# Pacing the gathers of the third and fourth batch on GpSimd by steps of the turn

## The reference

```python
x = x + tanh(g_xattn[0]) * L0_xattn(ctx, layernorm(x), ...)
x = x + tanh(g_ffn[0]) * L0_ffn(layernorm(x), ...)        # 64 experts, 8 per token
x = x + tanh(g_xattn[1]) * L1_xattn(layernorm(x), ctx, ...)  # 16 heads, causal
x = x + tanh(g_ffn[1]) * L1_ffn(layernorm(x), ...)        # 8 experts, 2 per token, and a shared one
```

```python
out = sum_j w8[token, j] * expert_out[row_of(token, j)]
```

## The kernel before

| step | engine, line | reports |
|---|---|---|
| normed input flipped, copied to XB | PE L707, ACT L947 | e_xt |
| queries, high part copied | PE L714, ACT L952 | e_hi_q |
| queries spread over the rows, copied to QS | PE L626, ACT L957 (two), DVE L1411 (two) | e_qs, 4 a turn |
| maxima of the scores, 8 units | PE L729 to L732, DVE L1417 | e_max |
| 16 heads: scores | PE L757 to L759 | e_s2 |
| 16 heads: exponentials | ACT L970 | e_exp, 16 a turn |
| average of 4 heads, four times | PE L747 | e_av |
| sums copied to OS | ACT L972 | e_os |
| flipped, divided | PE L768, DVE L1434, L1437 | e_ot, e_ont |
| flipped, copied to ON | PE L776, ACT L977 | e_on |
| output projection, added | PE L781, DVE L1446 | e_y, e_x3 |
| normed output flipped, copied to XB3 | PE L796, ACT L984 | e_xt3 |

## Time and profile before

### The profile page before, as it was taken

One profiled execution on the slowest core, in us unless ns is written; L12 is line 12 of the kernel. 1 busy time (PEld: TensorE's weight loads), 2 busy tenths in 40 slices (PEclk: granted clock), 3 DMA queues, 4 the chain that ended last, 5 costly groups with the idle time before them and its releaser, 6 DMA issues.

```text
span 597.7 us, 9231 instructions
## 1 busy us (share of the span) xinstructions
PE 424.5 (71%) x2738; PEld 356.9 (60%) x2738; DVE 345.3 (58%) x1053; ACT 185.0 (31%) x377; POOL 147.2 (25%) x156
## 2 busy tenths in 40 slices
PE   5353643303999999997137727899588988898796
PEld 3232532203998889985125514797368966886686
DVE  4897865395344444442357812488546976492664
ACT  4112210101233333433611412525235172526431
POOL 4117676572000000002776370000720000000000
PEclk9998565555999999998557775799878998899999
DMA  7997222175799999994332130000310000000000
GB/s 249 425 410 323 90 97 80 70 278 171 214 305 321 321 312 326 378 399 145 105 89 72 35 100 9 1 2 5 96 45 18 1 2 0 18 1 3 2 18 19
DMA packets 36789, 82.96 MB, mean 139 GB/s; under 512 B 6032, under 2 KB 16144, under 8 KB 34960
## 3 DMA queue, kind: packets, MB, share of 16 engines
q1 hardware_dynamic: 22896, 55.83, 26.8%
q0 software_dynamic: 6144, 16.79, 8.7%
q10 hardware_dynamic: 7712, 9.90, 4.6%
HBM read 50.44 MB, written 31.92 MB: 138 GB/s over the span
## 4 chain that ended last, share of the span: by engine, by line
PE 54%; issue 13%; DVE 12%; POOL 7%; ACT 6%; another core or an unknown queue 4%; DMA 3%; SPq 1%; DVEq 0%; POOLq 0%; ACTq 0%
PE PS L563 11%; PE PS L573 7%; POOL slots_in L439 6%; PE PS L652 5%; PE PS L626 3%; PE PS L550 3%; PE PS L729 2%; PE PS L665 2%; PE PS L666 2%; PE PS L667 2%; PE PS L781 2%; DVE WORK L1069 2%; DVE TOP L1065 2%; PE PS L714 2%
## 5 line engine op out<-in xcount | busy, mean ns | idle before, releaser
L449 POOL DMA_INDIRECT GB<-slots_out,IDXG x64 | 68.8, 1074 | 213.1 <-SPq L367 139.8
L563 PE MATMUL PS<-XTE,WR 128*128 128x128 f32 (+2 forms) x512 | 80.4, 301 | 0.0
L439 POOL DMA_INDIRECT slots_in<-XNA,IDX x64 | 64.9, 1014 | 39.0 <-issue 31.3
L563 PEld LDWEIGHTS PS<-XTE,WR 128*128 128x128 f32 x512 | 71.3, 195 | 0.3 <-ACT XTE L875 0.2
L1257 DVE TENSOR_TENSOR HE<-SGE,PS 128x128 f32<-128x128 f32 (+2 forms) x64 | 19.9, 311 | 68.1 <-ACT SGE L884 64.9
L573 PE MATMUL PS<-WR,HE 128*80 128x256 f32 (+2 forms) x198 | 53.3, 380 | 0.3 <-DVE HE L1257 0.3
L665 PE MATMUL PS<-XH,WGH 128*128 128x256 f32 x160 | 51.3, 320 | 0.0
L875 ACT COPY XTE<-PS 128x256 f32<-128x256 f32 (+2 forms) x64 | 26.3, 410 | 73.4 <-PE PS L550 73.4
L652 PE MATMUL PS<-WD,XW 128*128 128x256 f32 x160 | 43.5, 396 | 5.8 <-DVE TH L1335 5.8
L550 PE MATMUL PS<-CF,XE 80*128 80x80 f32 (+2 forms) x198 | 28.5, 257 | 26.2 <-DMA XE<-slots_in 26.2
L666 PE MATMUL PS<-XL,WGH 128*128 128x256 f32 x160 | 45.9, 287 | 0.0
(11 more groups left out here) (226 smaller groups left out, 825.0 us busy)
## 6 DMA issues: line engine op xcount, KB each, us to landing
WR<-in_wexp SPq DMA_DIRECT2D x64, 384.0 KB
slots_in<-GB SPq DMA_DIRECT2D x12, 1024.0 KB, 18.1
XE<-slots_in SPq DMA_DIRECT2D x24, 160.0 KB, 4.4
slots_out<-OE ACTq DMA_DIRECT2D x24, 160.0 KB, 4.3
XE<-slots_in SPq DMA_DIRECT2D x29, 128.0 KB, 4.6
slots_out<-OE ACTq DMA_DIRECT2D x29, 128.0 KB, 4.9
WGU<-in_wgu SPq DMA_DIRECT2D x1, 2560.0 KB
XE<-slots_in SPq DMA_DIRECT2D x11, 192.0 KB, 3.6
```

The lines of the kernel that those rows point to most:

```text
L439: pool.indirect_dma_start(out=xs, out_offset=bass.IndirectOffsetOnAxis(ap=IDX[:, t, j:j + 1], axis=0), in_=XNA[:, t, :], in_offset=None, b ...
L449: pool.indirect_dma_start(out=GB[:, t % BT, j, :], out_offset=None, in_=ys, in_offset=bass.IndirectOffsetOnAxis(ap=IDXG[:, t, j:j + 1], ax ...
L563: last = mm(psGE[place % 2][:, a, 0:cap(place)], W13[:, k, a, :], XTE[:, place % 2, k, 0:cap(place)], start=(k == 0), stop=(k == KC - 1))
```

## The change

The change gives `gather` an optional function that is called before every second of its 8 DMAs. For batches 2 and 3 it makes GpSimd wait for a step of the turn. Batches 0 and 1 are issued as before.

| pair of DMAs | first tile of batch b waits for | second tile waits for |
|---|---|---|
| 0 | (as before: gb_used) | XB3 copied, turn b-2 (and gb_used) |
| 1 | 8 exponentials of turn b-2 | XB copied, turn b-1 |
| 2 | OS copied, turn b-2 | high part of the queries copied, turn b-1 |
| 3 | ON copied, turn b-2 | QS complete, turn b-1 |

```diff
-            def gather(t):
+            def gather(t, pace=None):
                 for j in range(TOP0):
+                    if pace and j % 2 == 0:
+                        pace(t, j // 2)
                     pool.indirect_dma_start(out=GB[:, t % BT, j, :], out_offset=None, in_=ys,
...
+            def pace(t, pair):
+
+                at = t // BT - 2
+                if t % BT == 0:
+                    if pair == 1:
+                        pool.wait_ge(S["e_exp"], at * NH + NH // 2)
+                    elif pair == 2:
+                        pool.wait_ge(S["e_os"], at + 1)
+                    elif pair == 3:
+                        pool.wait_ge(S["e_on"], at + 1)
+                elif pair == 0:
+                    pool.wait_ge(S["e_xt3"], at + 1)
+                elif pair == 1:
+                    pool.wait_ge(S["e_xt"], at + 2)
+                elif pair == 2:
+                    pool.wait_ge(S["e_hi_q"], at + 2)
+                else:
+                    pool.wait_ge(S["e_qs"], (at + 1) * 4 + 4)
...
-                    gather(b * BT + i)
+                    gather(b * BT + i, pace if b >= 2 else None)
```

## The result

| | time, us (lowest to highest, runs) | ratio to before, 95% |
|---|---|---|
| before | 600.24 (598.06 to 602.74, 4) | |
| changed | 570.74 (565.74 to 577.02, 4) | 0.950 [0.945, 0.956] |

The later runs put a condition on this result: the kernel before takes 591 to 600 us in three sittings (a sitting is one round of runs on one chip) and 566 to 567 us in four others, and in one of those four the changed kernel was timed too, with no gain.

The account below looks back on a forecast made before the run. TensorE reports late beside unbroken gathers were taken to bound turns 0 and 1. Savings 14.6 + 8.2 less 8.3 that stays gave 14.5 us, so 599.5 became 585.0, forecast 586 at the median; range 577 to 597 us.

Parts of the forecast that it names:

- the place and the mechanism: Turns 0 and 1: TensorE's work is reported 2 to 8 us late while gathers stream; ceiling 22.8 us.
- signs asked for: Changed profile: paired gathers, turn 0 remote waits about 3 us, turn 1 near 31 us, no combine waiting for a DMA.
- Term 4: Seven pairs per batch moved later: cost 0, with about 11 us of slack before combine needs them.
- term 3: Lateness that stays: 2.5 us in turn 0, 2 in turn 1, 3.8 for 12 lone pairs; 8.3 us.
- Rival A: Relief nearly complete: pairs cause no lateness, only turn 1's four in a row cost 2 us; 579 us, chance 0.18.
- Terms 1 and 2: Stalls beside gathers in turn 0 (14.6 us) and turn 1 (8.22 us); ceiling of both 22.8 us.
- term 1: Turn 0, tenth exponential to copy of OS: 19.73 us against 5.09 in turn 2; ceiling 14.6 us.
- C (610): Slower: each separate pair makes one report late by about 2 us, 32 us against 22.8 saved; 610 us, chance 0.09.
- D (593): Half the relief: turn 0's fours still stall 4.7 us, single pairs cost 0.64 in full, colder clock; 593 us, chance 0.15.
- Rival B: No change: each gather costs 0.71 us anywhere, or a first pass through code is slow; 600.6 us, chance 0.08.

Follow-up runs that it names:

- c1_before: The kernel before itself, unchanged, profiled in a sitting without late reports; 566.1 us.
- c1_after: The changed kernel itself, run in a sitting without late reports; 567.0 us, 1.001 of the kernel before.
- b2_batch2_only: The changed kernel with only batch 2 paced and batch 3 issued in one run; 565.9 us, 0.999 of the kernel before.
- d1_batch2_only: The changed kernel with only batch 2 paced, run again in another sitting; 567.2 us, 1.001 of the kernel before.
- b3: The changed kernel with a batch's second pair of gathers released at the 16th exponential instead of the 8th; 569.7 us, 1.006 of the kernel before.
- f1_batch2_only: The changed kernel with only batch 2 paced, run again in another sitting; 566.5 us, 1.001 of the kernel before.
- a1: The kernel before, gathers left in place, with scratch clears ahead of each pair in batches 2 and 3; 576.9 us, 0.972 of the kernel before.
- a2: The kernel before, with each of batches 2 and 3 issuing its 16 gathers unbroken behind XB3's copy; 599.2 us, 1.009 of the kernel before.
- a3_plain_pool: The kernel before, with the gathers of batches 2 and 3 replaced by plain same-size DMAs on GpSimd's queue, fetching other rows; 564.6 us.
- e1_plain_slow: The kernel before, with batches 2 and 3 fetched by plain GpSimd DMAs, each followed by a scratch clear; 576.5 us, 0.975 of the kernel before.

## Why the prediction was right or wrong

**Right, for a late sitting: the place and the mechanism.** The time lay in TensorE's reports beside unbroken runs of gathers, and spacing them gave it back. That before and changed were both timed in a late sitting was luck: the prediction has no word of a kernel that takes 566 us unchanged. All signs asked for in turns 0 and 1 were there: pairs released by ScalarE or VectorE, "remote" gone from turn 0 (about 3 us were expected to stay), turn 2's combine without a wait for a DMA. Turn 1's heads take 26.6 us where near 31 were forecast, and the stretches behind the heads became shorter, not longer.

**Term 4 (moves cost 0): right.** The second tile's pairs ran at 360.8 to 377.6, even earlier than the 379 to 396 of the forecast, since the turn itself is shorter. No combine waits for a gather, and the context copy behind the last pair (377.6) is long over when the keys of turn 1 need it.

**The step that failed is term 3, "what stays": 8.3 us forecast, about 0 measured.** It gave each lone pair half of the 0.64 us that the first two gathers of turn 1 cost, and each group of four 2 to 2.5 us. Turn 1's heads with 8.71 us of gathers take 0.06 us longer than turn 2's with none. The 0.64 us wasn't the price of a pair. It may have been the beginning of a run: turn 1's group of four leaves 1.3 us of waits, all hidden. Rival A had this right, and its 579 was too high by the clock of the next point (5.6 us) and the 2 it kept for turn 1's four.

**Terms 1 and 2: the waits were read rightly, and the clock was put at nothing.** What late reports cost can be priced from the same kernel without them. The stretches of four profiles, us (c1_before and c1_after are from a sitting without late reports):

| | before | c1_before | c1_after | changed |
|---|---|---|---|---|
| up to the first exponential | 334.8 | 329.9 | 329.9 | 335.4 |
| heads of turn 0 | 43.4 | 24.9 | 24.4 | 24.0 |
| to turn 1 | 33.0 | 33.1 | 33.0 | 32.3 |
| heads of turn 1 | 36.4 | 26.5 | 29.4 | 26.6 |
| to turn 2 | 33.3 | 33.2 | 33.4 | 32.0 |
| heads of turn 2 | 28.2 | 28.2 | 26.6 | 26.6 |
| to turn 3 | 33.2 | 33.2 | 31.8 | 31.8 |
| turn 3 and tail | 55.3 | 55.3 | 55.4 | 55.2 |
| span | 597.7 | 564.3 | 563.8 | 563.9 |

Between the first two columns, one and the same kernel, the difference is 18.5 us in turn 0 and 9.9 in turn 1, together 28.4 and not 22.8 (and 4.9 more ahead of the turns: the changed kernel's own first exponential is as late as that of before). The medians agree: 600.2 against 566.1 to 566.8, less the 4.9, is 28.5 to 29.2.

Turn 0 divides at the copy of OS. Before it lie 26.93 and 11.72 us: 15.2 of difference, close to term 1's 14.6. The other 3.3 us lie behind it, where no report is late. The kernel before, then c1_before:

```profile
361.76:378.24 16.48, 12.63 (x48) 9.00 (x48) 6.29 (x22) 4.63 (x5) 0.39 (x1) 0.69 0.00 0
341.63:354.83 13.20, 8.66 (x48) 6.45 (x48) 6.95 (x22) 4.74 (x6) 9.48 (x11) 1.00 0.34 100
```

The same 48 matmuls are busy for 12.63 us at a granted clock of 0.69 and for 8.66 at 1.00. In turn 1 the yardstick was off in the same way: turn 2, 28.22 us at 0.94, was taken as undisturbed, and c1_before's turn 1 takes 26.54 at 1.00. The forecast had 0.86 and 0.94 before it in the earlier trace rows and priced neither; turn 0's clock it didn't read.

Whether the stalls pulled the clock down isn't shown. Behind OS in turn 0 it differs as much without any late report. One kernel, b2_batch2_only and then d1_batch2_only:

```profile
340.45:353.14 12.69, 8.65 (x48) 6.43 (x48) 6.11 (x22) 4.63 (x5) 4.00 (x4) 1.00 0.15 41
341.11:360.17 19.06, 15.43 (x48) 11.37 (x48) 6.11 (x22) 4.63 (x5) 3.98 (x4) 0.55 0.09 28
```

So 28.4 is the price against one undisturbed execution. From the first exponential of turn 0 to that of turn 2 the kernel before takes 146.1 us, and seven profiles without late reports in the turns and without clears (changed, c1_before, c1_after, b2, b3, d1 and f1_batch2_only) take 114.9 to 122.2: 24 to 31 us, the waits' 22.8 and a clock that varies. With 28.4 and nothing kept for term 3 the forecast would have been 599.5 - 28.4 + 1.1 = 572. Of its 15.3 us of error term 3 is 8.3, firmly; the clock is about 5.6.

**The rest of the 33.8 us between the two profiled executions goes with the clock too.** The last column is 5.9 us better in the turns than c1_before, which has no late report either. Windows over the heads of turn 1 and turn 2 in c1_before, then in c1_after:

```profile
387.88:414.42 26.54, 23.35 (x198) 18.87 (x199) 19.27 (x61) 13.52 (x26) 16.25 (x16) 1.00 0.25 72
447.63:475.85 28.22, 25.04 (x198) 20.12 (x199) 19.25 (x61) 13.52 (x26) 0.00 (x0) 0.94 0.00 1
```

```profile
387.25:416.65 29.40, 26.20 (x198) 21.09 (x199) 19.25 (x61) 13.52 (x26) 8.72 (x8) 0.88 0.13 38
450.05:476.61 26.56, 23.36 (x198) 18.89 (x199) 19.25 (x61) 13.52 (x26) 0.00 (x0) 1.00 0.00 1
```

The same 198 matmuls take 26.5 us where the upper level (2.4 GHz) is granted throughout and 28.2 or 29.4 where part of the stretch is at the lower (1.2 GHz), once in one turn and once in the other, with gathers or without. Such differences come from execution to execution and can't be put down to the change; the changed kernel's profiled execution, 565.7, lies 5.0 us under the median of its runs. The gain of the medians, 29.5, is the 28.4 of the late reports within 1.1.

**Rivals C (610) and D (593)** fell with the result; two terms of D's sum, 3 and 1 us, have no row behind them. **Rival B (no change)** was given 0.08. As a cause it fell in late sittings (a1 and a2 against each other). As an outcome it holds in the one sitting without late reports in which the changed kernel was timed (1.001), and would in three more where the kernel before takes 566 us, for a reason that none of my cases had: there is no stall to remove. One profile and three times within 0.5% gave no hint of that; it would have taken a second sitting of the kernel before.

**The bounds of the range.** The low end, 577, was A's. With the 5.6 us in it the end would have been near 571, at the measured median.

By their ratios no kernel that fetches the right rows beats the changed one in a late sitting, nor before in the other sittings. The change costs nothing measurable there (1.001 [0.997, 1.005], one sitting), so it is worth keeping.

## What to carry to other kernels

Time a kernel in several sittings before explaining a stall by its instructions, and look in each trace for a row that tells the sittings apart; an effect of 5% can belong to the sitting. Where unbroken indirect DMAs on GpSimd stand beside a serial chain of TensorE's reports, break them into pairs released by steps of the chain: here this cost nothing measurable when reports were on time. When a stall is to be removed, give the clock of the matmuls around it a term of its own, with a range taken from several profiles.

## What the runs showed of the hardware

- In some sittings waits of ScalarE and VectorE for TensorE last up to 9.6 us (a2_moved_run; the recorded end of L628 lies 10.45 us back there), beside unbroken runs of 16 indirect DMAs (0.99 to 1.4 us each, one every 1.3 us). Such a wait is "remote" in the profile. The sign of such a sitting is in 7 of 20 profiles, all of three sittings of seven. In the kernel before's late execution a run of 32 such DMAs at another place (279.55 to 324.37) went with no late report.
- TensorE's granted clock differs between executions of the same code without any late report: 0.88, 0.94 or 1.00 over the same 198 matmuls, 29.4, 28.2 or 26.5 us; 0.55 or 1.00 over the same 48, 19.1 or 12.7 us.
- In the late sittings the traces lack about a seventh to a fifth of the semaphore events (6219 to 6786 against 7801 to 7849).
- The same pieces by plain DMAs, with the same 6144 packets on the same queue, take 0.55 us each to issue and go with no late report (a3_plain_pool, e1_plain_slow).
- GpSimd's instructions hold up some short VectorE instructions. The same step of the norm in e1_plain_slow, where it ends at 406.26, just behind a plain DMA's issue and a clear (405.15 to 406.23), and then in the changed kernel, where GpSimd does nothing:

```profile
405.19 1.07 DVE L1049 TENSOR_SCALAR RS<-RS 128x2 int32<-128x2 int32 x1
```

```profile
403.43 0.17 DVE L1061 TENSOR_SCALAR RS<-RS 128x2 int32<-128x2 int32 x1
```

  The trace agrees here with the Trainium skill (SBUF — State Buffer, "Who interferes with whom"), by which VectorE's two-port forms and GpSimd lock each other out for whole instructions. This may be part of why the spaced and slowed kernels cost up to 1.4% in sittings without stalls; the clock is another part. In a1_spaced turn 0's stretch behind OS takes 16.98 us at 0.70, in the changed kernel 12.69 at 1.00.
